# A decoder layer on one core: where the products of one-hot blocks and weights are computed in the feed-forward stage

## What is computed

```python
q = einsum('bnd,de->bne', x, w_q); q = batch_norm(q)
sim = einsum('pbnhd,hkpd->pbnhk', q, keys)           # 2 x 8 heads x 32 keys a token
sx, ix = top_k(sim[0], 8); sy, iy = top_k(sim[1], 8)
all_scores = sx[..., :, None] + sy[..., None, :]     # 64 a head
scores, pk = top_k(all_scores, 8)
indices = (ix * 32 + iy) at pk                       # 8 heads x 8 experts of 1024, a token
h = einsum('bnd,bnhkd->bnhk', x, down_embed[indices])
h = softmax(scores) * gelu(h)
out = einsum('bnhk,bnhkd->bnd', h, up_embed[indices])
x = layernorm(x + out)
```

## Time and profile before

| what | value |
|---|---|
| time, median of 3 runs | 1376.27 us (1375.0 to 1378.77) |
| the profiled execution | 1373.3 us, of which the span of its instructions is 1371.5 us |
| busy: TensorE, VectorE, ScalarE, GpSimd | 1176.9, 1116.3, 849.1, 618.9 us |
| chain that ended last, largest lines | VectorE oneh L1427 4%, TensorE L1516 4% and L1517 3% of the span |
| expert rows, L1516 | 832 matmuls, TensorE idle just before them 44.9 us, mostly until VectorE's mv_lo |

### The profile page before, as it was taken

One profiled execution on the slowest core, in us unless ns is written; L12 is line 12 of the kernel. 1 busy time (PEld: TensorE's weight loads), 2 busy tenths in 40 slices (PEclk: granted clock), 3 DMA queues, 4 the chain that ended last, 5 costly groups with the idle time before them and its releaser, 6 DMA issues. The chain is left out here.

```text
span 1371.5 us, 32769 instructions
## 1 busy us (share of the span) xinstructions
PE 1176.9 (86%) x13174; PEld 923.8 (67%) x13174; DVE 1116.3 (81%) x2700; ACT 849.1 (62%) x994; POOL 618.9 (45%) x445
## 2 busy tenths in 40 slices
PE   3567999998999999999999999999997547777788
PEld 2454677776777767777776777677775526776678
DVE  5886888887889888897888888888885278999984
ACT  0347778877778786777778778887773531222121
POOL 2254856566475666656476575667230000000000
PEclk9768999999999999999999999999998665666656
DMA  7016999999999999999999999999997200000000
GB/s 150 1 38 131 193 199 198 190 196 194 195 188 197 195 191 197 196 189 192 201 195 194 194 193 196 191 190 190 188 190 139 69 1 1 5 5 5 5 5 6
DMA packets 695185, 191.77 MB, mean 140 GB/s; under 512 B 681045, under 2 KB 692601, under 8 KB 694905
## 3 DMA queue, kind: packets, MB, share of 16 engines
q1 hardware_dynamic: 695032, 189.67, 81.5%
HBM read 18.92 MB, written 0.82 MB: 14 GB/s over the span
## 5 line engine op out<-in xcount | busy, mean ns | idle before, releaser
L1003 PE MATMUL ps<-pT,xa_hi 128*128 128x128 f16 (+1 forms) x2496 | 415.9, 217 | 27.2 <-DMA pT<-p 26.9
L999 PE MATMUL ps<-pT,xa_hi 128*128 128x128 f16 (+1 forms) x2496 | 417.5, 217 | 21.4 <-ACT uT L840 20.1
L823 ACT ACTIVATE e<-ps,bias 128x1444 f32<-128x1444 f32 (+1 forms) x208 | 305.4, 1468 | 194.4 <-DVE bias L889 194.1
L887 DVE TENSOR_REDUCE nmax<-ps 128x1 f32<-128x1444 f32 (+1 forms) x208 | 344.5, 1656 | 95.3 <-PE ps L985 94.2
L1000 PE MATMUL ps<-pT,xa_lo 128*128 128x128 f16 (+1 forms) x2496 | 417.6, 217 | 0.0
L831 ACT ACTIVATE p<-e 128x1444 f16<-128x1444 f32 (+1 forms) x208 | 294.5, 1416 | 8.5 <-DMA pT<-p 0.5
L896 DVE TENSOR_TENSOR p<-e,p 128x1444 f16<-128x1444 f32 x144 | 268.1, 1862 | 11.4 <-ACT p L831 7.8
L999 PEld LDWEIGHTS ps<-pT,xa_hi 128*128 128x128 f16 x2496 | 242.8, 98 | 49.4 <-issue 33.6
L785 POOL TENSOR_TENSOR p<-e,p 128x1444 f16<-128x1444 f32 x64 | 187.5, 2930 | 180.3 <-ACT p L831 178.4
L1003 PEld LDWEIGHTS ps<-pT,xa_hi 128*128 128x128 f16 x2496 | 242.7, 98 | 34.1 <-DMA pT<-p 33.8
L1000 PEld LDWEIGHTS ps<-pT,xa_lo 128*128 128x128 f16 x2496 | 242.7, 98 | 13.1
(11 more groups left out here) (219 smaller groups left out, 1794.9 us busy)
## 6 DMA issues: line engine op xcount, KB each, us to landing
raw<-in_ctx SPq DMA_DIRECT2D x16, 704.0 KB
pT<-p SPq DMA_TRANSPOSE x416, 4.5
f_wq<-in_L_ffn_w_q SPq DMA_DIRECT2D x1, 1024.0 KB, 4.9
f_wqt<-in_ffn_wq_t SPq DMA_DIRECT2D x2, 512.0 KB, 7.0
x_tok<-in_x SPq DMA_DIRECT2D x1, 800.0 KB
out_x<-ost SPq DMA_DIRECT2D x6, 128.0 KB, 1.8
wk_t<-in_wk_t SPq DMA_DIRECT2D x1, 512.0 KB, 5.9
wq_t<-in_wq_t SPq DMA_DIRECT2D x1, 512.0 KB, 8.2
```

Source lines behind the costliest of these rows:

```text
L823: act.activation(e32[t % E_BUF][rows, :], score_banks(t)[rows, 0:T], ACT.Exp, bias=bias[rows, t % N_BUF:t % N_BUF + 1]).then_inc(e_done, 1)
L887: dve.tensor_reduce(nmax[rows, k:k + 1], score_banks(t)[rows, 0:T], AX_X, ALU.max, negate=True).then_inc(max_done, 1)
L999: pe.matmul(out, hi, ph, start=n == 0, stop=False)
L1003: last = pe.matmul(out, hi, pl, start=False, stop=n == NTILE - 1)
```

## The change

The two products mv_hi and mv_lo move from VectorE to GpSimd (new function `weighted_blocks`, called for each step after `combine` and `norm_rstd`). VectorE's order becomes eqc, w_lo, oneh. ScalarE reads cT out before rT. Two semaphores are new: `eqc_done` (raised by eqc, waited for by GpSimd) and `mv_done` (raised by mv_lo, waited for by TensorE's expert rows, and by ScalarE and VectorE before they write the operands of the next step). `wlo_done` is now raised once a step, and `oneh_done` by oneh itself.

```diff
+        eqc_done, mv_done = sem("feqc_done"), sem("fmv_done")
...
+            def weighted_blocks(i):
+                nh, w = step_shape(i)
+                j, nb = nh * HK, nh * NC
+                pool.wait_ge(eqc_done, i + 1)
+                pool.wait_ge(selT_done, 3 * i + 3)
+                if i:
+                    pool.wait_ge(g_ps, group_number(i, 0))
+                pool.tensor_tensor(out=mv_hi[0:j, 0:nb, 0:w], in0=eqc[0:j, 0:nb, 0:w],
+                                   in1=w_hi[0:j, 0:w].rearrange("p (a s) -> p a s", a=1).to_broadcast([j, nb, w]), op=ALU.mult)
+                pool.wait_ge(wlo_done, i + 1)
+                pool.tensor_tensor(out=mv_lo[0:j, 0:nb, 0:w], in0=eqc[0:j, 0:nb, 0:w],
+                                   in1=w_lo[0:j, 0:w].rearrange("p (a s) -> p a s", a=1).to_broadcast([j, nb, w]), op=ALU.mult).then_inc(mv_done, 1)
...
                 if i >= 2:
                     norm_rstd(i - 2)
+                weighted_blocks(i)
...
                     act.wait_ge(oneh_done, i)
+                    act.wait_ge(mv_done, i)
+                act.activation(cT[0:j, 0:w], ps[0:j, 4, P:P + w], ACT.Identity, bias=off8[0:j, 0:1]).then_inc(selT_done, 1)
                 act.activation(rT[0:j, 0:w], ps[0:j, 4, 0:w], ACT.Copy).then_inc(selT_done, 1)
-                act.activation(cT[0:j, 0:w], ps[0:j, 4, P:P + w], ACT.Identity, bias=off8[0:j, 0:1]).then_inc(selT_done, 1)
...
                 dve.wait_ge(selT_done, 3 * i + 1)
                 if i:
+                    dve.wait_ge(mv_done, i)
+                dve.tensor_tensor(out=eqc[0:j, 0:nb, 0:w], in0=iota_c[0:j, 0:nb, 0:w],
+                                  in1=cT[0:j, 0:w].rearrange("p (a s) -> p a s", a=1).to_broadcast([j, nb, w]), op=ALU.is_equal).then_inc(eqc_done, 1)
+                dve.wait_ge(selT_done, 3 * i + 3)
+                dve.tensor_tensor(out=w_lo[0:j, 0:w], in0=ps[0:j, 4, 2 * P:2 * P + w], in1=w_hi[0:j, 0:w], op=ALU.subtract).then_inc(wlo_done, 1)
+                if i:
                     dve.wait_ge(g_ps, group_number(i, 0))
                 dve.tensor_tensor(out=oneh[0:j, :, 0:w], in0=iota_w[0:j, :, 0:w],
-                                  in1=rT[0:j, 0:w].rearrange("p (a s) -> p a s", a=1).to_broadcast([j, P, w]), op=ALU.is_equal)
-                dve.wait_ge(selT_done, 3 * i + 3)
...
-                ins.then_inc(oneh_done, 1)
+                                  in1=rT[0:j, 0:w].rearrange("p (a s) -> p a s", a=1).to_broadcast([j, P, w]), op=ALU.is_equal).then_inc(oneh_done, 1)
...
                     pe.wait_ge(oneh_done, i + 1)
+                    pe.wait_ge(mv_done, i + 1)
...
-                    pe.wait_ge(wlo_done, 2 * i)
+                    pe.wait_ge(wlo_done, i)
```

## The result

The changed kernel is slower: 1412.18 us (median of 4 runs, 1408.24 to 1413.76) against 1376.36 us for the kernel before; the ratio is 1.0254, with a 95% interval of 1.0226 to 1.0282. The forecast was 1411. The profiled execution took 1410.64 us, its span is 1407.6 us.

The account below looks back on a forecast made before the run. VectorE's 12.66 us before the expert rows and TensorE's 25.5 us were taken to bound each step in turn. Six full steps add 34.2 us, the seventh 0.6; 34.8 on the 1376.27 median gives 1411, range 1392 to 1420.

Parts of the forecast that it names:

- VectorE's stretch before the expert rows counts in full: Feed-forward step: any change to the 12.66 us from rT to the first expert row moves the end; shortening counts up to 7.5.
- The products exclude the comparison: GpSimd's mv_hi and mv_lo and VectorE's oneh run one after another, +5.7 us a full step; chance 0.84.
- first rival: Packed 16-bit oneh leaves GpSimd room and they overlap: -2.16 us a step, 1363 us; chance 0.09.
- One product takes 4.07: One 2048-element product on GpSimd lasts 4.07 us, from the row nearest in count and types; 3.6 to 4.5 believed.
- The two orders of the race cost 18.32 and 18.47: TensorE's expert rows start 18.32 us after ScalarE's first read if GpSimd's mv_hi beats oneh, 18.47 if VectorE is first.
- The seventh step adds 0.6 us: Last step, of 64 tokens: TensorE's rows start at 1355.1 instead of 1354.5, GpSimd's mv_hi going before oneh.
- Nothing beside is late, and TensorE's longer idle costs nothing more: Feed-forward steps: comb is there by 20.5 us, before it is needed; TensorE's expert rows keep their pace at either clock.
- The time, 1411: Whole kernel: 34.8 us added to the median of three runs, 1376.27, gives 1411; from the profiled execution, 1408.1.
- The chances: Stated odds for the changed kernel: faster 0.09, same 0.04, slower 0.87.
- The releaser would be GpSimd: Changed trace: TensorE's idle before the expert rows is 13 us a step and ended by GpSimd.
- The far lower bound of the forecast: Far end for one GpSimd product: a fill that reads nothing, 1.84 us for 2048 elements, adding 1.2 us a step.
- The second rival: Exclusion is not whole, or GpSimd is much quicker on 16-bit data: 1383 or 1391 us; mixed case, chance 0.07.

Follow-up runs that it names:

- e2: Changed kernel with GpSimd filling mv_hi and mv_lo with a constant instead of multiplying, so it reads nothing: 1361.34 us, ratio 0.9902 to the kernel before.
- e7: Kernel before with both products ahead of oneh, all on VectorE, and oneh cut into four comparisons, each expert-row group awaiting its own: 1364.77 us, ratio 0.9943.
- e3: Changed kernel with oneh taking its column from PSUM instead of rT, leaving it one SBUF input: 1414.95 us in one run.
- e8: Changed kernel with GpSimd copying eqc into mv_hi and mv_lo instead of multiplying, so it reads one tile: 1383.37 us in one run.
- e4: Changed kernel with GpSimd waiting for w_lo before its first product, so that VectorE's oneh starts first: 1413.61 us in one run.
- e1: Changed kernel with both products back on VectorE, ahead of oneh, keeping only the new order: 1374.48 us, ratio 1.0002 to the kernel before.

## Why the prediction was right

Step by step, as it was put:

- *VectorE's stretch before the expert rows counts in full.* Shown from both sides: e2 and the change moved the rows' start by -2.18 and +5.65, and the time from the first read to the end by -13.7 and +34.7, about six times that. e7 shows where this stops: once VectorE is the bound, an earlier start gives under a third (10.4 us for six times 6.31).
- *The products exclude the comparison.* Shown. The trace had it for float32 alone; the 16-bit comparison, the case without a row, behaves like the others. e2, e3 with the search beside mv_lo, and e8 narrow the cause down to VectorE with two SBUF inputs against a GpSimd instruction that reads SBUF. The sentence of the Trainium skill that supported this (SBUF — State Buffer, Who interferes with whom), including that a GpSimd instruction which only writes is free, agrees with 8.68 in e2, 17.21 and 4.07 in e3 and 10.38 in e8. The narrower rule of the Trainium skill that stood with the first rival (Advanced Engine Details and Errata, VectorE Performance Modes) does not cover this case: by it the two would have overlapped, and oneh lasts 12.57 instead of 8.69.
- *One product takes 4.07.* It takes 4.06 (12.50 with the wait). The row with one 32-bit input was the right price for two 16-bit ones.
- *The two orders of the race cost 18.32 and 18.47.* The changed kernel has 18.31 and e4 18.43. GpSimd won six of seven races, by 0.04 us.
- *The seventh step adds 0.6 us.* Its rows start at 1389.94, 0.60 after add_experts ended at 1389.34, though VectorE won the race there, which the working had the other way round. But from that step's first read to the end the changed kernel needs 25.1 instead of 23.6, 1.5 more. Of the other 0.9, 0.3 lies in TensorE's work ahead of the rows, and 0.6 behind their start, 17.6 instead of 17.0. In e1, with no product on GpSimd, it is 17.6 as well, so nothing there points to the products; the cause stays open. The full steps add 33.1 instead of 34.2, so that the sum, 34.7 against 34.8, is right with two small errors of opposite sign.
- *Nothing beside is late, and TensorE's longer idle costs nothing more.* In the second step comb ends 20.27 after the first read (20.5). The granted clock of TensorE's stretch from the rows' start to the next first read is 0.52 instead of 0.58 there, nearer the lower of its two levels (0.50, 1.2 GHz) in both kernels, and the stretch lasts 25.51 against 25.50.
- *The time, 1411.* That the median is only 1.2 from it is luck, since the runs of either kernel spread over 4 to 6 us. The two profiled executions lie 37.3 apart: 34.7 of that in the stage, 1.4 ahead of its first read and 1.2 outside the span.
- *The chances.* Added up from the cases, they are 0.03 for the same time and 0.88 for slower, where 0.04 and 0.87 are stated; nothing hangs on it.
- *The releaser would be GpSimd.* Only in the first step does the profile say so; in the others it says "issue", since the expert rows wait for two semaphores.

## What to carry to other kernels

Work moved to GpSimd "beside" a VectorE instruction ran beside it here only where VectorE had at most one input in SBUF (e3, and the search beside mv_lo), or where GpSimd only wrote (e2). That is shown for tensor_tensor and MAX8 on VectorE and for products, copies and fills on GpSimd; other forms were not tried. Before such a move, look in the trace for a pair of the two engines whose recorded times already overlap, and compare ends, not durations: an instruction that ends its own length after the other one was waiting. Where an engine waits for one long instruction, cutting that into the pieces in which its result is used (e7) needs no other engine.

## What was not expected

The far lower bound of the forecast, a fill, was a bound of another kind: at 1.80 us for 2048 elements it isn't just cheaper than a product, it doesn't clash at all, and a copy of 1.89 us does. The second rival's price for such a short instruction, 1383 at 1.84 us, is what the copies took, 1383.37.
